# Placing the shift rows of half the heads with two DMAs of four partitions in place of eight DMAs of one partition

## What is computed

```python
# first block: 16 heads of 8 features, for each of the 32 sequences
q, k, v = split_heads(x @ Wq), split_heads(x @ Wk), split_heads(x @ Wv)
qc, kc = q - q.mean(-1), k - k.mean(-1)
cov = einsum('bhsd,bhtd->bhst', qc, kc) / D
var_comp = var(q)[..., :, None] * var(k)[..., None, :] / D
attn = softmax(cov + var_comp, axis=-1)
out = merge_heads(einsum('bhst,bhtd->bhsd', attn, v)) @ Wo
# second block: layer norm, causal attention of 16 heads along the 32 sequences,
# layer norm, router (top 2 of 8 experts), and all eight experts (128 -> 256, gelu -> 128) weighted by gates
```

## Time and profile before

| | |
|---|---|
| median of three runs | 1481.61 us (1475.91 to 1487.62) |
| the profiled execution's own time | 1485.91 us |
| its span | 1484.1 us |
| PE busy in the span | 1282.3 us (86%) |
| DVE, ACT, POOL busy | 989.7, 815.6, 375.6 us |
| mean granted clock of TensorE | 0.834 |
| DMAs of the changed line | 512 of 1 KB |

### The profile page before, as it was taken

One profiled execution on the slowest core, in us unless ns is written; L12 is line 12 of the kernel. 1 busy time (PEld: TensorE's weight loads), 2 busy tenths in 40 slices (PEclk: granted clock), 3 DMA queues, 4 the chain that ended last, 5 costly groups with the idle time before them and its releaser, 6 DMA issues.

```text
span 1484.1 us, 33659 instructions
## 1 busy us (share of the span) xinstructions
PE 1282.3 (86%) x11462; PEld 723.7 (49%) x11462; DVE 989.7 (67%) x2827; ACT 815.6 (55%) x1440; POOL 375.6 (25%) x644
## 2 busy tenths in 40 slices
PE   1788888888888888888887689999999999999998
PEld 1333433343333333333332256666666666666667
DVE  3765555665655556565554478888888888888774
ACT  0245444554545445454545556666676667677744
POOL 5524233342424334242411011111111111111000
PEclk9986566776757767676675689999999999999999
DMA  3000000000000000000000000000000000000000
GB/s 83 5 13 12 13 11 11 11 11 15 8 15 11 11 11 11 15 8 15 12 13 16 25 16 23 23 19 16 14 16 21 21 21 21 21 21 21 15 9 15
DMA packets 50965, 24.91 MB, mean 17 GB/s; under 512 B 6496, under 2 KB 50400, under 8 KB 50912
## 3 DMA queue, kind: packets, MB, share of 16 engines
q1 hardware_dynamic: 50912, 24.21, 6.0%
HBM read 15.28 MB, written 8.39 MB: 16 GB/s over the span
## 4 chain that ended last, share of the span: by engine, by line
PE 57%; ACT 15%; issue 9%; SPq 8%; DVE 6%; DMA 3%; POOL 1%; ACTq 1%; DVEq 0%; POOLq 0%
PE bank L550 51%; SPq L1483 7%; ACT Kexp L1368 6%; ACT hmid L1443 3%; DMA QKT<-shiftT 3%; PE bank L591 3%; DVE smax L1039 2%; ACT shiftT L1353 1%; PE bank L566 1%; ACT prob L1379 1%; PE bank L668 1%; DVE prob L1043 1%; ACT oT L1305 1%; ACT prob L1346 1%; ACT feat L1317 1%
## 5 line engine op out<-in xcount | busy, mean ns | idle before, releaser
L961 DVE TENSOR_REDUCE rowmin<-bank 128x2 f32<-128x512 f32 x512 | 345.8, 689 | 298.9 <-PE bank L550 298.1
L1346 ACT ACTIVATE prob<-bank 128x512 f32<-128x512 f32 x512 | 302.7, 599 | 383.9 <-PE bank L550 382.7
L550 PE MATMUL bank<-QKT 32*128 32x256 f16 x2048 | 252.8, 348 | 49.7 <-DMA QKT<-shiftT 40.0
L550 PEld LDWEIGHTS bank<-w_sb,hmid 128*128 128x128 f32 x2048 | 244.1, 192 | 24.4 <-issue 12.6
L550 PE MATMUL bank<-w_sb,hmid 128*128 128x128 f32 x2048 | 248.5, 276 | 0.5 <-issue 0.5
L1443 ACT ACTIVATE hmid<-bank,up_scale 128x512 f32<-128x512 f32 x256 | 176.2, 733 | 111.4 <-PE bank L550 111.2
L1368 ACT ACTIVATE Kexp<-bank,head_bias,head_mask 128x512 f32<-128x512 f32 x256 | 188.2, 848 | 42.5 <-PE bank L550 42.5
L550 PE MATMUL bank<-prob,V 128*25 128x256 f32 x2048 | 205.0, 535 | 0.0
L1251 DVE SCALAR_TENSOR_TENSOR acc<-bank,gate,acc 128x128 f32<-128x128 f32 x512 | 143.5, 343 | 73.0 <-PE bank L550 71.0
L550 PEld LDWEIGHTS bank<-QKT 32*128 32x128 f16 x2048 | 76.9, 104 | 222.3 <-issue 128.6
L434 POOL TENSOR_TENSOR sq<-feat 128x512 f32<-128x512 f32 x32 | 33.3, 1039 | 444.8 <-ACT feat L1317 227.5
(11 more groups left out here) (177 smaller groups left out, 1683.7 us busy)
## 6 DMA issues: line engine op xcount, KB each, us to landing
QKT<-shiftT SPq DMA_DIRECT2D x512, 1.0 KB
x_in<-in_L_attn_x SPq DMA_DIRECT2D x32, 128.0 KB, 2.1
z_scratch<-z_out SPq DMA_DIRECT2D x32, 128.0 KB, 1.9
xg<-in_L_attn_x SPq DMA_DIRECT2D x64, 64.0 KB, 1.9
zg<-z_scratch SPq DMA_DIRECT2D x64, 64.0 KB, 2.0
out<-acc SPq DMA_DIRECT2D x64, 64.0 KB, 1.6
w_sb<-in_L_ffn_w SPq DMA_DIRECT2D x1, 1024.0 KB, 6.2
wo<-in_L_attn_Wo SPq DMA_DIRECT2D x16, 4.0 KB
```

The costliest lines, as they stand in the source:

```text
L550: return pe.matmul(o, l, r, start=start, stop=stop, skip_group_check=True)
L961: dve.tensor_reduce(rowmin[h // 8][:, :, h % TILE_ROWS, h // TILE_ROWS % HALF], row_scores[i % 3][:].rearrange("p (s t) -> p s t", s=ST), ...
L1346: act.activation(prob[:, h % 8].rearrange("p t s -> p (t s)"), col_scores[h % 2][:], ACT.Exp, scale=exp_register).then_inc(s_exp, 1)
```

## The change

The tile `shift` gets its axes in another order, with the two parts outside the four heads of a quad. Its transpose then has the rows of part 0 in partitions 0 to 7 and those of part 1 in 8 to 15. So one DMA takes eight rows of `shiftT` and writes four partitions of `QKT` that lie 32 apart, two rows into each. A half is placed by two DMAs of 4 KB instead of eight of 1 KB. The counts that PE and ACT wait for follow from `SHIFT_DMAS`.

```diff
-SHIFT_DMAS = TILE_ROWS * SPARTS
+SHIFT_DMAS = SPARTS
...
-        shift = [sb(f"shift{k}", [P, ST, TILE_ROWS, SPARTS, HALF], F16) for k in range(2)]
+        shift = [sb(f"shift{k}", [P, ST, SPARTS, TILE_ROWS, HALF], F16) for k in range(2)]
...
-                                       shift[k][:, st].rearrange("p r j g -> p (r j g)"), identh[:])
+                                       shift[k][:, st].rearrange("p j r g -> p (j r g)"), identh[:])
...
-                dve.tensor_scalar(shift[k][:, :, :, 0, :], rowmin[k][:], 1.0 / UNIT, None, ALU.mult).then_inc(s_dve, 1)
+                dve.tensor_scalar(shift[k][:, :, 0], rowmin[k][:], 1.0 / UNIT, None, ALU.mult).then_inc(s_dve, 1)
...
-                    ins = dve.scalar_tensor_tensor(out=shift[k][:, st, :, 1, :], in0=rowmin[k][:, st],
-                                                   scalar=1.0 / UNIT, in1=shift[k][:, st, :, 0, :],
+                    ins = dve.scalar_tensor_tensor(out=shift[k][:, st, 1], in0=rowmin[k][:, st],
+                                                   scalar=1.0 / UNIT, in1=shift[k][:, st, 0],
...
-                for r in range(TILE_ROWS):
-                    for j in range(SPARTS):
-                        row, src = ROWS * r + SHIFT + j, (r * SPARTS + j) * HALF
-                        sp.dma_start(QKT[p][row:row + 1, 0, HALF * k:HALF * (k + 1), :],
-                                     shiftT[k][src:src + HALF, :]).then_inc(s_shd[k], 16)
+                for j in range(SPARTS):
+                    sp.dma_start(QKT[p][SHIFT + j:P:ROWS, 0, HALF * k:HALF * (k + 1), :],
+                                 shiftT[k][j * TILE_ROWS * HALF:(j + 1) * TILE_ROWS * HALF, :]).then_inc(s_shd[k], 16)
```

## The result

The kernel with two DMAs for each half takes 1428.38 us as the median of three runs (1419.49 to 1437.55), against 1481.61 before: a ratio of 0.963, with a 95% interval of 0.954 to 0.973. The profiled execution took 1419.49 us with a span of 1417.7, where that of before had 1485.91 and 1484.1.

A forecast was written before the change was run, and what follows sets the result against it. PE waiting for half 1's placement, mostly its issue time, was taken as the bound. Stall 22 to 26 us, clock echo some 17 and ends 5 make 47 us off 1481.6, rounded to 1436; range 1408 to 1477.

The forecast's parts named there:

- What ended last: Ahead of head 8, half 1's placement, including its issue time, ends last; PE began 1.66 us after finishing head 7.
- The price of issue and landing: Four-partition DMA: issue 0.56 us plus gap, landing 1.55 to 2.1 us; hidden while the placement stays under 4.2 us.
- The count of the waits: PE's waits for the placement: 31.1 us in 26 waits in the 27 steps, of which 22 us would be saved.
- What is late next: At head 8, the projection then waits for ACT's oT_all; 1.0 us of the 1.66 us is kept.
- The line of the clock: A step without a long stall takes 18.0 us plus 0.34 us for each us at 1.2 GHz.
- the closed form of the prediction: Step without stall takes 18.0 / (1 - 0.68 x (1 - clock)): 22.8 us at 0.69, saving 26 us over 27 steps.
- The echo in the clock: In the 27 steps, mean clock rises from 0.69 to 0.72, giving some 17 us beyond the stall itself.
- The ends: Waits at the start and in the last steps, outside the 27 steps, together give 5 us.
- A: Without the stall the steps' clock stays up: 1409 down to 1320 us; chance 0.10.
- B: Steps settle at a low clock, 24.0 us at 0.64, gaining about 0.1 us each: 1476 us; chance 0.13.
- C: Slower: all steps like the one of 24.99 us at clock 0.59, 27 us more: 1509 us; chance 0.03.
- D: SyncE's issue time goes by rows moved, so the placement doesn't get shorter: 1481 us; chance 0.04.

The follow-up runs named there:

- four_dmas: The two-DMA kernel with four DMAs of two partitions for each half instead of two: 1416.01 us, ratio 0.957 to the kernel before.
- idle_behind: The two-DMA kernel with six additional DMAs of 2 KB, read by nobody, issued behind each half's two real ones: 1427.33 us, ratio 0.960.
- idle_ahead: The two-DMA kernel with six additional DMAs of 2 KB, read by nobody, issued ahead of each half's two real ones: 1517.2 us, ratio 1.024.
- layout_only: The kernel before with only the new axes of the tile shift, still eight DMAs of one partition for each half: 1481.37 us, ratio 0.998.
- half1_two: The two-DMA kernel with half 0 back at eight DMAs and half 1 at two: 1431.76 us, ratio 0.963 to the kernel before.
- before_swapped: The kernel before, eight DMAs per half, with ACT's copy of half 1's shift moved ahead of its copy of oT: 1480.48 us, ratio 1.000.
- swapped_half0_eight: The two-DMA kernel with half 0 at eight DMAs and ACT's copy of half 1's shift ahead of that of oT: 1401.4 us, ratio 0.943.
- swapped: The two-DMA kernel with ACT's copy of half 1's shift ahead of its copy of oT in head 2: 1304.97 us, ratio 0.882.
- filled: The two-DMA kernel with additional matmuls in PE's waits, three ahead of the V projection, two ahead of slot 11's transposes: 1337.12 us, ratio 0.904.
- swapped_filled: The two-DMA kernel with ACT's new copy order, plus one additional matmul in slot 3 and two in slot 11: 1358.03 us, ratio 0.917.
- before_filled: The kernel before with four additional matmuls behind head 7, where PE waits for half 1: ratio 1.015, shorter runs 1497.67 and 1505.90 us.

## Why the prediction was right, step by step

**What ended last.** Shown. The wait ahead of head 8 hung on the issue of the placement, and it is gone with the issues (four_dmas, idle_behind) and comes back with them (idle_ahead).

**The price of issue and landing.** 0.56 us was taken for an issue, 0.534 came, and a landing of 1.64 us (from the last issue at 319.73 in idle_ahead, which has the same DMAs) where 1.55 was taken. The bounds didn't matter, since the deadline of 4.2 us is far. four_dmas stays within it, and eight issues miss it.

**The count of the waits.** One slip: of the 26 waits, 31.1 us, the last (0.29 us at 735.79) lies behind the 27 steps. In them there are 25 waits, 30.8 us. It changes nothing in the sum.

**What is late next.** `oT_all`, as said, with 0.7 us in each step: 19.9 us in all.

**The line of the clock.** The step without a long stall was put at 18.0 us and 0.34 us for each one at 1.2 GHz, from two steps of before. The steps of the kernel after, by the windows above: at 1.00 it gives 18.0 for 17.95; at 0.91 (3.5 us at the low clock) 19.2 for 19.35; at 0.83, 20.4 for 20.54; at 0.76, 21.5 for 21.50; at 0.64, 23.9 for 23.97; at 0.59, 25.0 for 24.95. The line also tells stall and clock apart in the experiments, to a few tenths of a microsecond, as long as the work in a step is the same. In the table, "line" is 18.0, or 17.4 where ACT has the new order, plus 0.34 x the time at 1.2 GHz, and the last column is PE's wait for the placed rows from the view of the waits, for each step:

| kernel | mean step | clock | line | step less line | wait for placed rows |
|---|---|---|---|---|---|
| before | 23.78 | 0.69 | 23.0 | 0.8 | 1.14 |
| layout_only | 23.72 | 0.71 | 22.7 | 1.0 | 1.39 |
| idle_ahead | 24.88 | 0.71 | 22.9 | 2.0 | 2.31 |
| after | 21.75 | 0.75 | 21.7 | 0.0 | none |
| idle_behind | 22.08 | 0.74 | 21.9 | 0.2 | none |
| four_dmas | 21.90 | 0.75 | 21.7 | 0.2 | none |
| half1_two | 22.33 | 0.75 | 21.8 | 0.5 | 0.47 |
| before_swapped | 23.61 | 0.73 | 21.7 | 1.9 | 1.85 |
| swapped_half0_eight | 21.05 | 0.85 | 19.5 | 1.5 | 1.6 |
| swapped | 17.87 | 0.97 | 17.8 | 0.1 | none |
| filled | 18.89 | 0.94 | 18.8 | 0.1 | none |
| swapped_filled | 19.58 | 0.87 | 19.1 | 0.5 | none |
| before_filled | 24.18 | 0.82 | 21.0 | 3.2 | 1.8 |

The three last ones have additional work, and in before_filled it overran the wait, which the line doesn't know of.

**The sum.** Forecast 47 us below the median, measured 53 (66 between the profiles). By the closed form of the prediction, the stall was 27 x 0.98 = 26 us, as counted; by the line with the step's own length (the table) it was 27 x 0.8 = 22. The echo in the clock, which is what a better clock gives on top of the stall itself, was the term that was mis-sized between the profiles: I took a mean of 0.72 and some 17 us, it was 0.75, and 27 x (22.8 - 21.7) = 30 us. The ends gave 11 us and not 5, as the last steps went along with the clock (the step after 673.44 took 19.13 us at 0.91; its counterpart at 729.99 took 22.61 at 0.62). But 13 of the 66 us are scatter: the profile of after is of the fastest of its three runs, and that of before lies 4 us above its median. Against the medians the whole sum was 6 us short, and how much of that is the clock's is not shown.

That the total came so near is in part luck. The 0.72 was a choice among clocks seen in single steps and not worked out, and the reason given for it ("PE is less idle in the stretch in which the clock fell") is not borne out: with twice the stall the clock was 0.71 (idle_ahead), and with more work in PE's waits it once fell more often (swapped_filled). What the runs do show is that the profiles with the long stall in most steps, in ACT's old order and without additional matmuls, lie at 0.69 to 0.71 and those without it at 0.74 to 0.75.

**A step that was not wrong here, but would be one change further.** "The placement of half 0 ... has five heads of work between itself and its reader, and PE doesn't wait for it in the steps" held for the profile of before, because its heads 11 to 15 ran at 1.2 GHz. Then the cover was 7.6 us from the first issue; at 2.4 GHz it is 4.3, and eight issues with their landing need about 6 (half1_two; before_filled and swapped_half0_eight show the same wait). In the kernel after both halves are short, so it doesn't show.

**The rivals.** A at its full length (all steps at 2.4 GHz) didn't come from this change; single steps of it did, at 17.95 us, and with ACT's order it came nearly whole. B and C show as patterns of single steps (23.97 at 0.64, 24.95 at 0.59) that the kernel after still falls into, but doesn't stay in. B was priced wrongly: steps of 24.0 us would be 0.2 us longer than the mean of 23.78 and not 0.1 shorter, so all of them in that pattern would have given about 1483 us, outside the range. D is out by the issue times. The rule of the Trainium skill on the clock ("TensorE: Matmul & The Clock Gate", section "HAM oscillation — how this bites in real kernels") is borne out in part: the clock did rise as the wait for a DMA went away, but it goes on falling in most steps without any such wait. The sentence of the Trainium skill on issue time ("DMA: Bandwidth & Descriptors", section "Issuing engines are not separate DMA queues"), weighed in the prediction, is about a single DMA, and there the trace has 0.61 us from issue to issue against 1.55 to landing, 40% of it. The prediction's factor of nearly three sets seven issues against one landing. Eight small DMAs in one queue add up their issues, and that was the whole matter here.

**What stays open.** What brings the clock down within a step. It is not simply PE's idle time: additional matmuls raised the clock in two kernels (before_filled, filled) and lowered it in a third (swapped_filled), where PE was busy 466 us of 509. Nor is it the length of the stall for the placement (idle_ahead). I haven't tried which kind of additional work, or which place for it, does the one and which the other. Nor is it shown what part of the 123 us of the new order a given amount of shorter waiting would bring; there is only the one step of half a microsecond.

## What to carry to other kernels

Where a small transfer is placed by several DMAs, count the issues first: here eight issues took 4.8 us to the 1.55 us of the last one's landing, and one DMA with a stride over partitions costs no more to issue than one for a single partition. Saving issues pays up to the reader's deadline and nothing beyond it, so read the deadline from the timeline, and read it again at the clock that the kernel will have after the change. And where the granted clock of TensorE swings within each step, split the step's time into a fixed part, a part per microsecond at the low clock, and the waits: here that told a stall from its echo to a few tenths of a microsecond, and it showed how much there was to be had from the clock alone. It doesn't say what will move the clock.

## What was not expected of the hardware

Half a microsecond less of waiting in a step of 22 us (0.71 instead of 1.18 us ahead of the V projection) took the mean granted clock of the steps from 0.75 to 0.97 and the step from 21.75 to 17.87 us. Matmuls whose results nobody reads made a kernel 6% faster (1337 against 1428 us), and one step further 4% slower (1358 against 1305). The same program has steps of 17.95 and 24.95 us with the same instructions in them, sometimes one right after the other (17.96 and 24.93 from 143.83 on), and its runs differ by more than 1%.
